# A decoder layer on one core: value and turning steps of the first attention reordered, first weight remainders on GpSimd, and routing logits by token rows

## The chip, the cores and the metric

One core of a Trainium2 chip runs the whole kernel. The metric is the device time in microseconds of one execution; the kernel before took 1061.29, 1063.31 and 1063.31 us in three runs, a median of 1063.31 us.

## The reference

The input is 16 sequences of 128 tokens with 256 features. One layer is computed, in float32:

```python
x = layernorm(x + attention(x))                    # 16 heads of 16, softmax over 128 keys, projection wo
x = layernorm(x + recurrence(k=x, v=ctx, w, u))    # out_t = A + exp(u + k_t) * (v_t * B + max(t - 1, 0))
                                                   # A = exp(-w)*A + exp(k_t)*v_t ; B = exp(w)*B + exp(-k_t), from t = 1 on
x = layernorm(x + experts(x))                      # 8 experts, each with all 128 tokens of a sequence:
# logits = x @ Wg.T (8 columns); gate = softmax(logits); sum_e gate[e] * (gelu(x @ W1[e] + b1[e]) @ W2[e] + b2[e])
```

Top-k takes 128 of 128 tokens, so each expert works on every token, weighted by its gate.

## The kernel before, in words

The sequences are worked on in eight pairs. A pair goes through attention, recurrence and routing (the numbered steps 1 to 62 of the `attend` and `route` functions), and then through eight visits, one for each expert. A visit streams the expert's two weight matrices in and runs units: `up` (TensorE, L578) makes hidden values, `hidden` (ScalarE, L728) applies gelu, `hidden_hi` and `hidden_lo` split the result in two parts, and `down` (L601) multiplies by the second matrix. Every engine has its own program with the same loops, and works strictly in the order in which its program is written; engines meet at semaphores.

Float32 products are made of three matmuls of a high and a low part (`product`, L405 to L409). So everything that TensorE reads is split: ScalarE copies the high part, and an engine subtracts it from the source for the low part. For weights these are `split_hi` (ScalarE, L739) and `split_lo` (VectorE, by the helper `low` at L790).

The first pair has nothing to run beside it. Its steps stand in the list FIRST_ORDER. The attention goes in four quarters (u = 0 to 3), each with two groups of four heads: scores (L407 to L409), the maximum and its subtraction (VectorE L856, L863), the exponential (ScalarE L674), turning the probabilities with eight transposes (TensorE L458), their high part (ScalarE L681) and low part (VectorE L870), the product with the values (TensorE L478, L479), and their sum, reciprocal and scaling (VectorE L876, L878, L880). There is one buffer of turned probabilities, and they are turned into PSUM banks 2 and 3. So the turning of a quarter stands behind the value product of the quarter before it in TensorE's program.

After attention come the projection, the first norm (L889, L808), the turning of y1, the exponentials (ScalarE L692 to L696), the two scans (VectorE L828), the mixture (L909, L911, L915, L919, with one addition on GpSimd at L1098), the turning back (TensorE L534), the second norm, and routing: part 0 turns x2 and splits it, part 1 makes the logits, part 2 turns them and subtracts the maximum, part 3 is the softmax, parts 4 and 5 turn the gates and add the gated b2 (L957). Routing of the first pair up to part 3 stands ahead of visit 0; parts 4 and 5 stand in the items of visit 0, beside the first steps of pair 1.

A visit with one active pair has 4 units and 8 items (three `up`, then `down` and `up` by turns); visit 0 is such a one, and the first 40 items carry the attention, recurrence and routing of pair 1, the next 48 those of pair 2. In each item an engine does the unit's part, then its steps of the next pair, then its splits of the coming weights. Seven of the eight weight pieces of visit 0 (all four of w1, three of w2) are split ahead of visit 0: ScalarE after steps Y1 and REC, VectorE at the same places.

SyncE issues all loads in one queue: 12 pieces at the start, then x and context of pair 1, then each further piece when the low part of the piece in its buffer is made.

The functions that the change touches:

## Time and profile before

| | us |
|---|---|
| runs | 1061.29, 1063.31, 1063.31 (median 1063.31) |
| profiled execution | 1064.93 |
| its span in the trace | 1063.2 |
| TensorE matmul busy | 946.8 |
| VectorE busy | 757.0 |
| ScalarE busy | 696.2 |
| GpSimd busy | 99.1 |

The profiled execution is 1.6 us above the median. Busy times are totals over stages with different limits: at the start, one engine after another works on the first pair; in the middle, TensorE is hardly ever idle.

### The profile page before, as it was taken

The numbers are of one execution on the slowest core, as the hardware profiler recorded it, in microseconds if no ns is written. First come the engines' busy times: TensorE is split into PE (matmuls) and PEld (weight loads), VectorE is DVE, ScalarE is ACT, GpSimd is POOL, SyncE is SP. The second block draws the span as 40 slices with busy tenths as digits, with TensorE's granted clock in tenths as the row PEclk, the third lists the DMA queues.
The fourth block names the chain that finished last, engine by engine and source line by source line (L and its number), as shares of the span: only waits on it lengthen the run. The fifth ranks groups of instructions, "written<-read, shape, count | busy, mean of one in ns | idle before, by whom it ended". The sixth has DMA issues, their size and how long they took to land.

```text
span 1063.2 us, 17552 instructions
## 1 busy us (share of the span) xinstructions
PE 946.8 (89%) x6480; PEld 850.4 (80%) x6480; DVE 757.0 (71%) x1526; ACT 696.2 (65%) x1231; POOL 99.1 (9%) x117
## 2 busy tenths in 40 slices
PE   6558687988799989999899989999899999999997
PEld 5447687878688878888798878988798888989997
DVE  6757768786688757787678758786678757655675
ACT  6347675665567766667677666677676665656775
POOL 2012001100120011100111001100011001000000
PEclk9669998999899999999999999999899999999999
DMA  6022233222122222222222222221222222232360
GB/s 200 11 70 89 90 109 100 80 60 70 51 80 71 79 70 80 67 83 80 70 90 70 71 90 63 69 88 61 79 80 80 61 69 80 87 112 90 103 186 11
DMA packets 89268, 86.40 MB, mean 81 GB/s; under 512 B 5960, under 2 KB 89184, under 8 KB 89184
## 3 DMA queue, kind: packets, MB, share of 16 engines
q1 hardware_dynamic: 89184, 85.29, 26.1%
q8 instruction: 52, 0.85, 0.3%
q14 instruction: 32, 0.26, 0.1%
HBM read 83.17 MB, written 2.10 MB: 80 GB/s over the span
## 4 chain that ended last, share of the span: by engine, by line
PE 65%; DVE 19%; ACT 11%; issue 4%; DMA 0%; POOL 0%; SPq 0%; ACTq 0%; POOLq 0%; DVEq 0%
PE up_ps L407 9%; PE up_ps L409 9%; PE up_ps L408 9%; PE down_ps L615 9%; PE down_ps L616 8%; PE down_ps L617 8%; DVE w_lo L790 4%; PE bank L407 3%; PE bank L408 3%; PE bank L409 3%; DVE h_lo L790 2%; ACT probs L674 2%; DVE pt_lo L870 2%; ACT L674 2%; DVE kd L820 1%
## 5 line engine op out<-in xcount | busy, mean ns | idle before, releaser
L728 ACT ACTIVATE h_all<-up_ps,b_all 128x512 f32<-128x512 f32 (+1 forms) x296 | 182.7, 632 | 292.6 <-PE up_ps L409 291.1
L615 PE MATMUL down_ps<-w_hi,h_hi 128*128 128x256 f32 x1024 | 299.9, 293 | 41.4 <-DVE h_lo L790 41.4
L790 DVE TENSOR_TENSOR w_lo<-w_raw,w_hi 128x512 fp32r<-128x512 f32 x296 | 206.1, 710 | 153.2 <-ACT w_hi L739 153.0
L616 PE MATMUL down_ps<-w_lo,h_hi 128*128 128x256 f32 x1024 | 293.7, 287 | 0.0
L617 PE MATMUL down_ps<-w_hi,h_lo 128*128 128x256 f32 x1024 | 293.6, 287 | 0.0
L615 PEld LDWEIGHTS down_ps<-w_hi,h_hi 128*128 128x128 f32 x1024 | 199.2, 194 | 54.1 <-DVE w_lo L790 39.7
L407 PE MATMUL up_ps<-x2t_hi,w_hi 128*128 128x512 f32 (+1 forms) x592 | 224.9, 380 | 0.0
L408 PE MATMUL up_ps<-x2t_lo,w_hi 128*128 128x512 f32 (+1 forms) x592 | 219.5, 371 | 0.0
L409 PE MATMUL up_ps<-x2t_hi,w_lo 128*128 128x512 f32 (+1 forms) x592 | 219.2, 370 | 0.0
L616 PEld LDWEIGHTS down_ps<-w_lo,h_hi 128*128 128x128 f32 x1024 | 200.0, 195 | 5.2
L790 DVE TENSOR_TENSOR h_lo<-h_all,h_hi 128x512 fp32r<-128x512 f32 x256 | 182.3, 712 | 27.6 <-ACT h_hi L719 27.6
L617 PEld LDWEIGHTS down_ps<-w_hi,h_lo 128*128 128x128 f32 x1024 | 199.9, 195 | 0.0
L739 ACT ACTIVATE w_hi<-w_raw 128x512 fp32r<-128x512 f32 x296 | 180.2, 628 | 0.7 <-PE down_ps L617 0.7
L719 ACT ACTIVATE h_hi<-h_all 128x512 fp32r<-128x512 f32 x256 | 160.8, 628 | 2.3
L409 PEld LDWEIGHTS up_ps<-x2t_hi,w_lo 128*128 128x128 f32 x592 | 114.6, 194 | 19.3
L407 PEld LDWEIGHTS up_ps<-x2t_hi,w_hi 128*128 128x128 f32 x592 | 116.2, 196 | 11.9
L408 PEld LDWEIGHTS up_ps<-x2t_lo,w_hi 128*128 128x128 f32 x592 | 116.2, 196 | 11.0
L1070 POOL TENSOR_TENSOR var_eps<-moments,eps_row 128x2 f32<-128x2 f32 x24 | 11.2, 466 | 667.3 <-DVE moments L801 667.3
L870 DVE TENSOR_TENSOR pt_lo<-bank,pt_hi 128x512 f16<-128x512 f32 x64 | 41.3, 684 | 30.0 <-ACT pt_hi L681 30.0
L972 DVE SCALAR_TENSOR_TENSOR acc<-down_ps,gate,acc 128x256 f32<-128x256 f32 x112 | 47.0, 475 | 13.1 <-PE down_ps L617 13.1
L820 DVE TENSOR_SCALAR kd<-k_both,head_mask 128x512 fp32r<-128x512 f32 x120 | 50.4, 478 | 0.0
L856 DVE TENSOR_REDUCE neg_max<-bank 128x4 f32<-128x512 f32 x58 | 38.1, 682 | 5.2 <-PE bank L409 5.2
(171 smaller groups left out, 1118.2 us busy)
## 6 DMA issues: line engine op xcount, KB each, us to landing
w_raw<-in_w_dram SPq DMA_DIRECT2D x296, 256.0 KB, 2.7
x_in<-in_x_dram SPq DMA_DIRECT2D x8, 256.0 KB, 3.0
ctx_sb<-in_ctx_dram SPq DMA_DIRECT2D x8, 256.0 KB, 3.1
out_dram<-acc SPq DMA_DIRECT2D x8, 256.0 KB, 3.2
w_raw<-in_wq_dram SPq DMA_DIRECT2D x1, 256.0 KB, 3.0
w_raw<-in_wk_dram SPq DMA_DIRECT2D x1, 256.0 KB, 4.2
w_raw<-in_wv_dram SPq DMA_DIRECT2D x1, 256.0 KB, 4.3
w_raw<-in_wo_dram SPq DMA_DIRECT2D x1, 256.0 KB, 4.6
```

The costliest lines, as they stand in the source:

```text
L407: nc.tensor.matmul(ps, hi, rhs_hi, start=first, stop=False)
L408: nc.tensor.matmul(ps, hi, rhs_lo, start=False, stop=False)
L409: return nc.tensor.matmul(ps, lo, rhs_hi, start=False, stop=last)
L615: nc.tensor.matmul(ps, hi, w2h[:, c, :], start=c == 0 and j == 0, stop=False, skip_group_check=True)
L616: nc.tensor.matmul(ps, hi, w2l[:, c, :], start=False, stop=False, skip_group_check=True)
L617: mm = nc.tensor.matmul(ps, lo, w2h[:, c, :], start=False, stop=c == FC - 1 and j == PAIR - 1, skip_group_check=True)
L719: nc.scalar.activation(h_hi[:, unit % HALF, :], h_all[:, unit % HALL, :], ACT.Copy).then_inc(h_hi_ready, 1)
L728: a = nc.scalar.activation(h_all[:, unit % HALL, k * wide:(k + 1) * wide], up_ps[unit % 2][:, k * wide:(k + 1) * wide], ACT.Gelu_apprx_tan ...
L739: nc.scalar.activation(piece((w1_hi, w2_hi)[i], i, q), raw(m, i), ACT.Copy)\
L790: return nc.vector.tensor_tensor(dst, src, hi.bitcast(F32), ALU.subtract)
L820: i = nc.vector.tensor_scalar(kd[:, :, :, h, :], k_both[:, :, c, :].rearrange("p a (j t) -> p a j t", j=PAIR), head_mask[:, h:h + 1], None ...
L870: nc.vector.tensor_tensor(pt_lo[:, i], by_head(bank[2 + i]), pt_hi[:, i], ALU.subtract)\
```

## The change

- Two buffers of turned probabilities (`pt_hi`, `pt_lo`). In the first attention odd quarters are turned into the PSUM banks `down_ps`, and the turning of each quarter stands ahead of the value product of the quarter before it. ScalarE's wait for the value product reaches back two quarters instead of one.
- The seven first weight splits: ScalarE's copies stand inside the first attention, and GpSimd does the subtractions.
- The addition of the recurrence that GpSimd made (L1098) is made by VectorE, for all pairs.
- Routing logits: the turned tokens become the stationary operand. For each of two sequences and two halves of the features there is one matmul with 16 moving columns (high and low part of Wg side by side) and one with 8 columns. The copy of the logits on ScalarE and their two transposes go; VectorE adds the two halves with one more reduction. This holds for all pairs.
- Parts 1 to 5 of the first pair's routing stand in items 1, 2, 3, 5 and 6 of visit 0, in the bank `down_ps[1]`. TensorE's wait for the b2 addition ahead of pair 1's values goes.
- Two memsets of padded Wg tiles go.

```diff
-        pt_hi = sb("pt_hi", [P, 2, HQ, S], F16)
-        pt_lo = sb("pt_lo", [P, 2, HQ, S], F16)
+        pt_hi = sb("pt_hi", [P, 2, 2, HQ, S], F16)
+        pt_lo = sb("pt_lo", [P, 2, 2, HQ, S], F16)
...
+        def route_bank(b, i):
+            return down_ps[1] if first(b) else bank[2 + i]
+        def turned(p, u):
+            return down_ps if first(p) and u % 2 else bank[2:4]
...
             def turn_probs(p, u):
+                if u == 1 and first(p):
+                    pe.wait_ge(shifted, 6)
...
-                    for kc in range(C):
-                        mm = product(bank[2][:, 0:TOK], wg_hi[:, kc, :], wg_lo[:, kc, :],
-                                     x2t_hi[:, kc, b % 3, :], x2t_lo[:, kc, b % 3, :], kc == 0, kc == C - 1)
-                    mm.then_inc(logits_t_ps, 1)
-                if part == 2:
-                    pe.wait_ge(logits_t_ready, b + 1)
                     for t in range(PAIR):
-                        mm = nc.tensor.transpose(bank[3][:, t * P:(t + 1) * P], logits_t[:, t * S:(t + 1) * S], ident[:])
+                        rows = slice(t * S, (t + 1) * S)
+                        ps = route_bank(b, 0)[:, t * 2 * E:(t + 1) * 2 * E]
+                        for kc in range(C):
+                            nc.tensor.matmul(ps, x2t_hi[:, kc, b % 3, rows], wg_both[:, kc].rearrange("p k e -> p (k e)"),
+                                             start=kc == 0, stop=False, skip_group_check=True)
+                            mm = nc.tensor.matmul(ps[:, 0:E], x2t_lo[:, kc, b % 3, rows], wg_both[:, kc, 0, :],
+                                                  start=False, stop=kc == C - 1, skip_group_check=True)
                     mm.then_inc(logits_ps, 1)
...
+                    if n == 0:
+                        for part in FIRST_ROUTE.get(k, []):
+                            route(0, part)
                     for p, s in steps(FIRST_ITEM[n] + k):
-                        if s in GATE_STEP:
+                        if s in GATE_STEP and p > 1:
                             route(p - 1, 4 + GATE_STEP.index(s))
...
-                            if u > 0:
-                                act.wait_ge(pv_ps, QUADS * p + (g - 1))
-                            nc.scalar.activation(pt_hi[:, i], by_head(bank[2 + i]), ACT.Copy).then_inc(pt_hi_ready, 1)
+                            if u > 1:
+                                act.wait_ge(pv_ps, QUADS * p + (g - 3))
+                            nc.scalar.activation(pt_hi[:, u % 2, i], by_head(turned(p, u)[i]), ACT.Copy).then_inc(pt_hi_ready, 1)
...
-                if part == 1:
-                    act.wait_ge(logits_t_ps, b + 1)
-                    nc.scalar.activation(logits_t, bank[2][:, 0:TOK], ACT.Copy).then_inc(logits_t_ready, 1)
...
                 if s == REC_STEP[3]:
+                    nc.vector.tensor_tensor(y1t[:], y1t[:], scan_a[:], ALU.add).then_inc(mix_a_ready, 1)
...
-                    lg = bank[3][:, 0:PAIR * P].rearrange("p (t e) -> p t e", t=PAIR)[:, :, 0:E]
-                    nc.vector.tensor_reduce(route_max[:], lg, AX_X, ALU.max, negate=True).then_inc(route_step, 1)
+                    halves = route_bank(b, 0)[:, 0:PAIR * 2 * E].rearrange("p (t k e) -> p t e k", t=PAIR, k=2)
+                    nc.vector.tensor_reduce(logits[:], halves, AX_X, ALU.add).then_inc(route_step, 1)
+                    dve.wait_ge(route_step, 5 * b + 1)
+                    nc.vector.tensor_reduce(route_max[:], logits[:], AX_X, ALU.max, negate=True).then_inc(route_step, 1)
...
-                if s == Y1_STEP:
-                    for q in range(G):
-                        split_lo(0, 0, q)
-                if s == REC_STEP[-1]:
-                    for q in range(G - 1):
-                        split_lo(0, 1, q)
...
-                if s == MIX_A_STEP:
-                    pool.wait_ge(xa_step, 6 * p + 3)
-                    pool.wait_ge(exps_ready, p + 1)
-                    nc.gpsimd.tensor_tensor(y1t[:], y1t[:], scan_a[:], ALU.add).then_inc(mix_a_ready, 1)
...
+            def split_lo(n, i, q):
+                m = sequence(n, i, q)
+                pool.wait_ge((w1_hi_ready, w2_hi_ready)[i], G * n + q + 1)
+                nc.gpsimd.tensor_tensor(piece((w1_lo, w2_lo)[i], i, q), raw(m, i), piece((w1_hi, w2_hi)[i], i, q).bitcast(F32),
+                                        ALU.subtract).then_inc((w1_ready, w2_ready)[i], 1)
...
-                EXP_STEP[0], EXP_STEP[1], TURN_STEP[0], EXP_STEP[2], SCORE_STEP[3], VALUE_STEP[0],
-                TURN_STEP[1], VALUE_STEP[1], EXP_STEP[3], TURN_STEP[2], VALUE_STEP[2], TURN_STEP[3], VALUE_STEP[3]]
-               + list(range(ATT_STEP, ROUTE_STEP[-1] + 1)))
+                EXP_STEP[0], EXP_STEP[1], TURN_STEP[0], EXP_STEP[2], SCORE_STEP[3], TURN_STEP[1],
+                VALUE_STEP[0], EXP_STEP[3], TURN_STEP[2], VALUE_STEP[1], TURN_STEP[3], VALUE_STEP[2], VALUE_STEP[3]]
+               + list(range(ATT_STEP, ROUTE_STEP[0] + 1)))
+FIRST_ROUTE = {1: [1], 2: [2], 3: [3], 5: [4], 6: [5]}
+FIRST_SPLIT = {EXP_STEP[1]: [(0, 0), (0, 1)], TURN_STEP[1]: [(0, 2), (0, 3)], EXP_STEP[3]: [(1, 0), (1, 1), (1, 2)]}
```

## Rows read from the trace of the kernel before

**Rows 1.** Busy time by engine (page, share of the span, instructions).

```profile
PE 946.8 (89%) x6480; PEld 850.4 (80%) x6480; DVE 757.0 (71%) x1526; ACT 696.2 (65%) x1231; POOL 99.1 (9%) x117
```

**Rows 2.** Busy time in a stretch: PE, PEld, DVE, ACT, POOL, granted clock, DMA share, GB/s.

```profile
30.00:42.00 12.00, 6.34 (x64) 5.13 (x64) 8.91 (x19) 4.08 (x8) 0.00 (x0) 0.55 0.01 3
```

**Rows 3.** Chain of waits, a turning in the first attention (start, length, what).

```profile
37.47 1.80 PE bank L458 x8
```

**Rows 4.** Timeline of VectorE in the first attention (start, length, what, idle before).

```profile
30.93 0.57 DVE L876 TENSOR_REDUCE pv_sum<-bank 128x136 f32<-128x408 f32 x1
...
31.99 1.28 DVE L870 TENSOR_TENSOR pt_lo<-bank,pt_hi 128x512 f16<-128x512 f32 x2
...
42.03 0.29 DVE L880 TENSOR_TENSOR att<-pv_sum,inv_sum 128x128 f32<-128x128 f32 x1
```

**Rows 5.** Timeline of ScalarE: turned probabilities, weight copies.

```profile
25.61 1.07 ACT L681 ACTIVATE pt_hi<-bank 128x512 f16<-128x512 f32 x2
...
44.88 2.18 ACT L739 ACTIVATE w_hi<-w_raw 128x512 fp32r<-128x512 f32 x4
```

**Rows 6.** Timeline of VectorE from the first norm to the second.

```profile
55.18 0.66 DVE L901 TENSOR_TENSOR inc_a<-exp_k,ctx_t 128x504 f32<-128x504 f32 x1
...
58.00 1.63 DVE L911 TENSOR_TENSOR exp_k<-exp_k,ramp 128x512 f32<-128x512 f32 x1
...
61.01 1.89 DVE L790 TENSOR_TENSOR w_lo<-w_raw,w_hi 128x512 fp32r<-128x512 f32 x3
```

**Rows 7.** Timeline of ScalarE, last of the exponentials' copies.

```profile
54.46 0.62 ACT L696 ACTIVATE y1t<-bank 128x512 f32<-128x512 f32 x1
```

**Rows 8.** GpSimd's subtraction of values, and its addition for pair 0.

```profile
20.47 1.16 POOL L1090 TENSOR_TENSOR v_all<-v_all,v_cat 128x512 f32<-128x512 f32 x1
...
57.32 1.77 POOL L1098 TENSOR_TENSOR y1t<-y1t,inc_a 128x512 f32<-128x512 f32 x1 [6.52 <-DVE inc_a L828]
```

**Rows 9.** VectorE beside GpSimd's addition of pair 2, and line 911's durations (min/median/max).

```profile
276.69 1.76 DVE L909 TENSOR_TENSOR exp_k<-ctx_t,inc_b 128x512 f32<-128x512 f32 x1
...
L911 DVE TENSOR_TENSOR exp_k<-exp_k,ramp x8: 691/693/1633, 58.0 to 889.4; 128x512 f32<-128x512 f32 x8
```

**Rows 10.** Timeline of TensorE from the first turning back to pair 1's first projection.

```profile
61.14 1.12 PE L534 MATMUL bank<-ident,exp_k 128*128 128x128 f32 x4 [8.39 <-DVE exp_k L919]
...
68.19 0.55 PE L407 MATMUL bank<-x2t_hi,wg_hi 128*128 128x256 f32 x1 [1.02 <-DVE x2t_lo L790]
...
75.43 0.36 PE L407 MATMUL bank<-xt_hi,proj_hi 128*128 128x256 f32 x1
```

**Rows 11.** Timeline of VectorE: the last small instruction of routing's part 3.

```profile
72.57 0.17 DVE L790 TENSOR_TENSOR gate_all<-gate,gate_all 128x16 fp32r<-128x16 f32 x1
```

**Rows 12.** VectorE in visit 0: the idle times at both ends of a full stretch.

```profile
80.69 0.69 DVE L790 TENSOR_TENSOR w_lo<-w_raw,w_hi 128x512 fp32r<-128x512 f32 x1 [4.21 <-ACT w_hi L739]
...
94.24 0.69 DVE L856 TENSOR_REDUCE neg_max<-bank 128x4 f32<-128x512 f32 x1 [0.59 <-PE bank L409]
```

**Rows 13.** ScalarE: a table load in visit 0 and its idle time ahead of pair 1's exponential.

```profile
87.62 1.28 ACT L674 ACT_TABLE_LOAD   x1
91.86 1.23 ACT L674 ACTIVATE probs<-probs 128x512 f32<-128x512 f32 x2 [2.95 <-DVE probs L863]
```

**Rows 14.** TensorE: transposes, and the value products with 51 and 34 columns.

```profile
23.49 1.04 PE L458 MATMUL bank<-ident,probs 128*128 128x128 f32 x8
...
28.22 0.18 PE L478 MATMUL bank<-v_cat,pt_hi 128*128 128x51 bf16 x1
28.25 0.18 PE L479 MATMUL bank<-v_cat,pt_lo 128*128 128x34 bf16 x1
```

**Rows 15.** Weight loads of pair 2's logits matmuls.

```profile
292.10 0.19 PEld L407 LDWEIGHTS bank<-x2t_hi,wg_hi 128*128 128x128 f32 x1
292.22 0.19 PEld L408 LDWEIGHTS bank<-x2t_lo,wg_hi 128*128 128x128 f32 x1
```

**Rows 16.** TensorE ahead of pair 2's turning back.

```profile
281.77 1.12 PE L534 MATMUL bank<-ident,exp_k 128*128 128x128 f32 x4 [4.46 <-DVE exp_k L919]
```

More of the change, by code:

```diff
@@ L457, in turn_probs @@
                     for h in range(HQ):
-                        mm = nc.tensor.transpose(by_head(bank[2 + i])[:, h, :], probs[:, u % 2, i, h, :], ident[:])
+                        mm = nc.tensor.transpose(by_head(turned(p, u)[i])[:, h, :], probs[:, u % 2, i, h, :], ident[:])
                     mm.then_inc(pt_ps, 1)
@@ L567, in route @@
                     for t in range(PAIR):
-                        mm = nc.tensor.matmul(by_tile(bank[3])[:, t, :], gate_t[:, t * S:(t + 1) * S], b2_all[:], start=True, stop=True)
+                        mm = nc.tensor.matmul(by_tile(route_bank(b, 1))[:, t, :], gate_t[:, t * S:(t + 1) * S], b2_all[:], start=True, stop=True)
                     mm.then_inc(b2_ps, 1)
@@ L774, in _ @@
                         hidden(n, u)
+                    if n == 0:
+                        for part in FIRST_ROUTE.get(k, []):
+                            route(0, part)
                     for p, s in steps(FIRST_ITEM[n] + k):
-                        if s in GATE_STEP:
+                        if s in GATE_STEP and p > 1:
                             route(p - 1, 4 + GATE_STEP.index(s))
@@ L956, in route @@
                     dve.wait_ge(b2_ps, b + 1)
-                    nc.vector.tensor_tensor(x2_all[:, b % 2], by_tile(bank[3]), x2_all[:, b % 2], ALU.add).then_inc(x2_biased, 1)
+                    nc.vector.tensor_tensor(x2_all[:, b % 2], by_tile(route_bank(b, 1)), x2_all[:, b % 2], ALU.add).then_inc(x2_biased, 1)
             def hidden_lo(n, u):
@@ L1003, in _ @@
             nc.vector.memset(ones[:], 1.0).then_inc(dve_setup, 1)
+            dve.wait_ge(dve_setup, 1)
+            nc.vector.tensor_tensor_scan(ramp[:], ones[:], ones[:], 0.0, ALU.mult, ALU.add).then_inc(dve_setup, 1)
             dve.wait_ge(dve_setup, 2)
-            nc.vector.tensor_tensor_scan(ramp[:], ones[:], ones[:], 0.0, ALU.mult, ALU.add).then_inc(dve_setup, 1)
-            dve.wait_ge(dve_setup, 3)
             nc.vector.tensor_scalar(ramp[:], ramp[:], -2.0, 0.0, ALU.add, ALU.max)
@@ L1013, in _ @@
                 attend(0, s)
-                if s == Y1_STEP:
-                    for q in range(G):
-                        split_lo(0, 0, q)
-                if s == REC_STEP[-1]:
-                    for q in range(G - 1):
-                        split_lo(0, 1, q)
                 if s == ATT_STEP:
@@ L1022, in _ @@
                     dve.wait_ge(masks_made, MASKS + 2)
-                    low(wg_lo[:, :, 0:E], wg_raw[:], wg_hi[:, :, 0:E])
-                    nc.vector.tensor_scalar(b2_rest[:], b2_raw[:], third[:, 0:1], None, ALU.mult)
+                    low(wg_both[:, :, 1, :], wg_raw[:], wg_both[:, :, 0, :])
+                    nc.vector.tensor_scalar(b2_raw[:], b2_raw[:], third[:, 0:1], None, ALU.mult)
                     nc.vector.tensor_scalar(third[:, 1:2], third[:, 0:1], -2.0, 1.0, ALU.mult, ALU.add).then_inc(dve_setup, 1)
                     dve.wait_ge(dve_setup, DVE_SETUP - 2)
-                    nc.vector.scalar_tensor_tensor(out=b2_all[:], in0=b2_hi[:].bitcast(F32), scalar=third[:, 1:2], in1=b2_rest[:],
+                    nc.vector.scalar_tensor_tensor(out=b2_all[:], in0=b2_hi[:].bitcast(F32), scalar=third[:, 1:2], in1=b2_raw[:],
                                                    op0=ALU.mult, op1=ALU.add).then_inc(dve_setup, 1)
@@ L1047, in _ @@
                         hidden_lo(n, order[k - 1][1])
+                    if n == 0:
+                        for part in FIRST_ROUTE.get(k, []):
+                            route(0, part)
                     for p, s in steps(FIRST_ITEM[n] + k):
-                        if s in GATE_STEP:
+                        if s in GATE_STEP and p > 1:
                             route(p - 1, 4 + GATE_STEP.index(s))
@@ L1125, in _ @@
                 attend(0, s)
+                for i, q in FIRST_SPLIT.get(s, []):
+                    split_lo(0, i, q)
             for n in range(VISITS):
```

40 lines of the change are left out of this document (16 added, 24 removed).

## The prediction

> **What bounds the kernel now.** I read the page's busy times first: TensorE is busy for 89% of the span, VectorE for 71%, ScalarE for 65% [rows 1]. That is an average. The table of stretches shows the other case: from 30 to 42 us TensorE works 6.3 of 12 us at a granted clock of 0.55, hence mostly at 1.2 GHz, and VectorE 8.9 [rows 2]. There one pair goes through its attention alone, and each engine waits for the next. The chain of waits shows eight transposes that take 1.80 us at this clock [rows 3]; they stand behind a value product, which stands behind VectorE's low part, so turning, copying and subtracting follow each other. All that follows is coupled by the written order of the items, and no engine waits for a weight load after the first 10 us. So what the first pair loses or gains, I take to move the end by as much.
>
> **First attention.** VectorE has no idle time to speak of up to 30.93, where the last subtraction of maxima ends, and its part ends with the scaling at 42.03+0.29 = 42.3 [rows 4]. In between it does four groups of sum, reciprocal and scaling, each 1.06 (30.93 to 31.99), and six low parts, 0.6 each: 4.2+3.6 = 7.8 us of work in 11.4 us. The reordered list takes the waits out, so VectorE could be done at 38.8. But ScalarE now does seven weight copies there, 0.54 each [rows 5]. I laid its program out by its own durations: copies from 25.6, the first turned copy at 26.7 (its reader VectorE comes at 27.35, no loss), then exponentials, two copies, exponentials, three copies, and so the third quarter's turned copy at 33.7, its first half ready at 34.3. VectorE is there at 33.2 and waits 1.1. End at 39.9. I add 0.1 for blocking by GpSimd (below): **gain 2.3**. Bounds: 3.5 (ScalarE hides it all) and 0.5 (VectorE is blocked too).
>
> **Weight remainders.** The four subtractions that VectorE did ahead of the scans bring nothing: the multiplication at 55.18 waits for ScalarE's last copy, which ends at 54.46+0.62 = 55.08 [rows 6, 7]. The three at 61.01, 0.6 each, keep the norm's statistics until 62.81 [rows 6]; the transposes that these need end at 61.14+1.12 = 62.26 [rows 10]. **Gain 0.5.** On GpSimd each costs 1.16 to 1.77 [rows 8]; seven fit between 26 and 37 us and nobody reads them before visit 0, 65 us at the earliest: zero on the path. Their buffers are free sooner, so SyncE's reloads, which waited for them in its one queue until 52, go from the context load (about 42) on; nothing waits for a load, so zero either way.
>
> **The recurrence's addition.** Line 911 takes 0.69 in the median but 1.63 in the first pair, while GpSimd's addition runs from 57.32 to 59.09; for pair 2 it is line 909, of the same form, that takes 1.76 [rows 8, 9]. One VectorE instruction is thus stretched by 0.94 to 1.08 in each pass. VectorE's own addition costs 0.60, the distance of such instructions. For the first pair that is a **gain of 0.34**. By this sum the logits' inputs are ready 2.3+0.5+0.34 = 3.1 us sooner. The Trainium skill (SBUF — State Buffer, Who interferes with whom) says the same in general: a VectorE instruction with two SBUF inputs and a GpSimd one lock each other out for a whole instruction. The rows agree, and the rule speaks against the seven subtractions beside the attention. What it would hit: VectorE's inputs there lie mostly in PSUM; only the scalings have two in SBUF. Two of four meet a subtraction, up to 1.16 each [rows 8]; the first of them falls mostly into the 1.1 us wait.
>
> **Start of visit 0.** Before, 7.24 us pass from the logits' matmul at 68.19 to pair 1's first projection at 75.43 [rows 10]. Now TensorE has: `up` 0, 12 matmuls at 1.2 GHz, 256/1.2 = 213 ns each, 2.56; four transposes at 0.225, 0.9 [rows 3]; `up` 1, a quarter at the low and the rest at the high level, 1.7; the new logits, 0.9. Sum 6.1, a **gain of 1.1** (0 if the clock stays low through `up` 1).
>
> **Routing inside visit 0.** In VectorE's program from 80.69 on the first idle time is at 94.24, 0.59 us [rows 12]. The small routing instructions, the last of which ran at 72.57 while it was idle otherwise [rows 11], now stand in that full stretch: 0.17 and some 0.03 of start each, the softmax part's six (one pair closer) 1.07, the maximum part with one more reduction 0.6. **Loss 1.67.** The b2 addition (0.6) falls into the idle 0.59, since TensorE waits there for the shifted scores: zero, or 0.6 without that cover. ScalarE must load its table for the exponential and again for gelu, 2x1.28+0.2 = 2.8 us; it has 2.95 us idle ahead of pair 1's exponential, where it waits for VectorE [rows 13], and it runs some 3 us ahead of VectorE at that item: zero, at most 2.8. TensorE's new wait for the gates (item 5) has pair 1's scores behind it, and these wait for VectorE's masked keys, made later still: zero.
>
> **Other pairs.** Each loses the 1.08 block and gets 0.60. For pairs 1 and 2 VectorE sets the pace (TensorE waits 4.46 us for it ahead of the turning back [rows 16]): 2x0.48, **gain 1.0**. For the last five TensorE is full, and I count 0.1 each, **gain 0.5** (0 to 2.4). The logits: out go six matmuls of 256 columns at 0.12 and two transposes at 0.11 (eight in 1.04, less the tail) [rows 14], 0.94; in come eight narrow ones. Their price isn't in the trace. From below: matmuls of 51 and 34 columns with 16-bit weights start 0.03 apart (28.22, 28.25); from above, the load of 0.19 and a matmul of 0.18 one after the other, 0.37 [rows 14, 15]. I take 0.11, the transposes' distance, as they too load 128 columns of float32 each time. 8x0.11 = 0.88, **gain 0.06 a pair, 0.4 in seven**. The copy that goes from ScalarE (0.39) and VectorE's extra reduction (0.2) lie beside full TensorE: zero.
>
> **Sum.** -2.3-0.5-0.34-1.1+1.67-1.0-0.5-0.4 = -4.4 us. The profiled execution had 1064.93 (span 1063.2), so 1060.5 against that; the median of the runs is 1.6 lower, 1063.31, and against it I forecast **1058.9**.
>
> **Rivals.**
>
> A. The narrow matmuls are cheap. For it: the 0.03 distance [rows 14]. Against: those weights have 16 bits, these 32. At 0.04 to 0.06, 64 of them bring 3.2 to 4.5 more: about 1055.
>
> B. VectorE is blocked by GpSimd in the first attention at two or more scalings [rows 8], behind ScalarE's late copies; 1.1 to 2.2 more on the path: 1060 to 1061.
>
> C. Visit 0 takes back more: the table loads aren't covered, or TensorE, waiting longer for keys, falls to 1.2 GHz and runs a `down` at 2.56 instead of 1.4. For it: this stage already shows waits on all engines. 2.2 more: 1061.1.
>
> D, slower. Each narrow matmul waits for its own load: 0.37 instead of 0.11. It decides in TensorE's full stages, in routing part 1. 64x0.26 = 17 us, so 1063.3-4.4+16.6 = 1075.5; it outweighs the rest from 0.11+4.4/64 = 0.18 a matmul on. Against it: the loads of the old logits start 0.12 apart beside running matmuls on the same rows of the array [rows 15], each 0.19 long, so they are hidden, and behind transposes of 128 columns they still are. The Trainium skill (TensorE: Matmul & The Clock Gate, The mechanism) has the rule behind this rival: a weight load overlaps running matmuls only when the row group differs. The rows here contradict it.
>
> E. No effect: the head's gain is real but is lost again in a later wait. Against: nothing later is tied to a fixed time.
>
> **How the numbers follow.** Forecast 0.48, A 0.15, B 0.14, C 0.14, D 0.05, E 0.04. About 0.2% (2.1 us) is what a measurement can tell from no change. Forecast, A, B and half of C are faster, 0.83 (I count a little off for what I missed: 0.82); the other half of C and E the same, 0.12; D and unnamed mishaps slower, 0.06. The range takes in A's middle and C: 1055.0 to 1062.0; left out are D, E and the ends.
>
> **What would show it.** The last scaling of the first attention ends near 40 us; VectorE waits about 1 us for the third quarter's turned copy; line 911 takes 0.69 in all eight passes, and no VectorE instruction 1.7 beside them; `up` 0 starts near 65, pair 1's projection near 71; VectorE's full stretch in visit 0 ends near 95 instead of 98; narrow matmuls start 0.11 apart. I am wrong if TensorE's busy time grows by over 5 us, if VectorE's scalings in the attention take 1 us and more, or if the start of visit 1 lies where it was.

## The result and the profile after

The changed kernel took 1054.41 us (median of four runs, 1053.62 to 1056.16), the kernel before in the same comparison 1062.8 us: a ratio of 0.9926, interval 0.9908 to 0.9943, which is 7.9 us less of 1063.3. Two later comparisons gave 0.9931 and 0.9926. I had forecast 4.4 us less. The direction was right, the size was not, and the time lies below my range (1055.0 to 1062.0). In the two later comparisons the medians of the changed kernel were 1056.57 and 1055.48 us, just inside the range, but the distance to the kernel before was the same 7.3 to 7.9 us. The profiled execution had 1053.62 us, span 1051.9. It is the lowest of its four runs, and that of before lies 1.6 above the median, so the two traces differ by 11.3 us where the medians differ by 8.4.

The page's busy times after, beside [rows 1]:

```profile
span 1051.9 us, 17529 instructions
PE 935.5 (89%) x6480; PEld 842.3 (80%) x6480; DVE 751.3 (71%) x1533; ACT 694.9 (66%) x1225; POOL 94.6 (9%) x116
```

TensorE's 946.8 us went down by 11.3, but such a total also counts how long the clock stayed low. So I go by places. The timeline of VectorE after, at the end of the first attention (start, duration, operation; in brackets the idle time before it and what ended it), answers to [rows 4]:

```profile
32.07 0.57 DVE L878 TENSOR_REDUCE pv_sum<-bank 128x136 f32<-128x408 f32 x1
32.92 1.24 DVE L882 TENSOR_TENSOR att<-pv_sum,inv_sum 128x128 f32<-128x128 f32 x1
34.08 1.27 DVE L872 TENSOR_TENSOR pt_lo<-bank,pt_hi 128x512 f16<-128x512 f32 x2
36.12 0.54 DVE L882 TENSOR_TENSOR att<-pv_sum,inv_sum 128x128 f32<-128x128 f32 x1
38.61 0.29 DVE L882 TENSOR_TENSOR att<-pv_sum,inv_sum 128x128 f32<-128x128 f32 x1
39.67 0.29 DVE L882 TENSOR_TENSOR att<-pv_sum,inv_sum 128x128 f32<-128x128 f32 x1
...
55.61 0.69 DVE L913 TENSOR_TENSOR exp_k<-exp_k,ramp 128x512 f32<-128x512 f32 x1
...
59.63 0.76 DVE L798 BATCH_NORM_STATS2 stats<-bank 128x6 f32<-128x256 f32 x2 [1.21 <-PE bank L538]
```

The last scaling ends at 39.96, where I had 39.9, but on another way. (In the two further traces of the changed kernel it ends at 38.79 and 39.03, since the attention starts 1.1 and 0.7 us sooner there; its length is the better measure, see run e5.) VectorE doesn't wait for the third quarter's copy at all: the low parts at 34.08 have no idle time before them. Instead the first scaling takes 1.24 instead of 0.29 and the second 0.54, and GpSimd's row says why:

```profile
26.24 2.52 POOL L1101 TENSOR_TENSOR w_lo<-w_raw,w_hi 128x512 fp32r<-128x512 f32 x2 [2.39 <-ACT w_hi L743]
30.27 6.24 POOL L1101 TENSOR_TENSOR w_lo<-w_raw,w_hi 128x512 fp32r<-128x512 f32 x5 [1.51 <-ACT w_hi L743]
```

Its five subtractions run back to back from 30.27 to 36.51, and both stretched scalings lie in there; those at 38.61 and 39.67 don't. One of my signs for being wrong has thus come: a scaling in the attention that takes 1 us and more. The second norm's statistics wait for TensorE's transposes now and no longer stand behind three subtractions: the step of 0.5 I had counted.

The start of visit 0 on TensorE, which answers to [rows 10]:

```profile
64.92 0.58 PE L410 MATMUL up_ps<-x2t_hi,w_hi 128*128 128x256 f32 x1 [0.93 <-DVE x2t_lo L792]
...
69.58 0.17 PE L556 MATMUL down_ps<-wg_both,x2t_hi 128*128 128x16 f32 x1
69.60 0.25 PE L558 MATMUL down_ps<-wg_both,x2t_lo 128*128 128x8 f32 x1
69.71 0.26 PE L556 MATMUL down_ps<-wg_both,x2t_hi 128*128 128x16 f32 x1
69.82 0.25 PE L558 MATMUL down_ps<-wg_both,x2t_lo 128*128 128x8 f32 x1
...
70.38 0.36 PE L410 MATMUL bank<-xt_hi,proj_hi 128*128 128x256 f32 x1
```

`Up` 0 starts at 64.92 (forecast near 65), the projection at 70.38 (near 71), and the narrow matmuls stand 0.11 apart. From `up` 0 to the projection it is 5.46 us, in two further traces of the changed kernel 6.57 and 6.80, where I had worked out 6.1. Then VectorE's full stretch, beside [rows 12]:

```profile
75.66 0.69 DVE L792 TENSOR_TENSOR w_lo<-w_raw,w_hi 128x512 fp32r<-128x512 f32 x1 [5.12 <-ACT w_hi L743]
...
92.40 1.89 DVE L792 TENSOR_TENSOR w_lo<-w_raw,w_hi 128x512 fp32r<-128x512 f32 x3
94.20 0.88 DVE L977 SCALAR_TENSOR_TENSOR acc<-down_ps,gate,x 128x256 f32<-128x256 f32 x2
...
101.59 0.58 DVE L878 TENSOR_REDUCE pv_sum<-bank 128x136 f32<-128x408 f32 x1
```

In the trace before, these four stand at 80.69, 96.05, 97.85 and 106.64. The lead is 5.03 us at the first and 3.65 at the accumulation: the routing in the stretch costs 1.38 there, near my 1.67. But at the sum of pair 1's values the lead is 5.05 again. Either the loss was given back, or the trace before lost as much in the same place; run e4 decides it.

### The profile page after: what moved, and what is told of

It reads as the page before. It is cut to its first block, busy times and chain, and to the rows that moved or that the text cites. A ratio compares the mean times of both kernels' runs of the same rounds, so it can differ in the third digit from the quotient of the medians.

```text
span 1051.9 us, 17529 instructions
## 1 busy us (share of the span) xinstructions
PE 935.5 (89%) x6480; PEld 842.3 (80%) x6480; DVE 751.3 (71%) x1533; ACT 694.9 (66%) x1225; POOL 94.6 (9%) x116
## 4 chain that ended last, share of the span: by engine, by line
PE 67%; DVE 17%; ACT 11%; issue 3%; DMA 0%; POOL 0%; SPq 0%; ACTq 0%; POOLq 0%; DVEq 0%
PE up_ps L410 10%; PE up_ps L412 10%; PE up_ps L411 10%; PE down_ps L619 9%; PE down_ps L621 9%; PE down_ps L620 9%; PE bank L410 3%; PE bank L411 2%; DVE w_lo L792 2%; PE bank L412 2%; DVE pt_lo L872 2%; ACT probs L681 2%; DVE h_lo L792 2%; ACT L681 2%; DVE kd L822 2%
## 5 line engine op out<-in xcount | busy, mean ns | idle before, releaser
L792 DVE TENSOR_TENSOR w_lo<-w_raw,w_hi 128x512 fp32r<-128x512 f32 x289 | 195.3, 688 | 151.4 <-ACT w_hi L743 151.1
L411 PE MATMUL up_ps<-x2t_lo,w_hi 128*128 128x512 f32 (+1 forms) x592 | 218.4, 369 | 0.0
L872 DVE TENSOR_TENSOR pt_lo<-bank,pt_hi 128x512 f16<-128x512 f32 x60 | 38.5, 684 | 26.0 <-ACT pt_hi L688 26.0
```

Source lines behind the costliest of these rows:

```text
L411: nc.tensor.matmul(ps, hi, rhs_lo, start=False, stop=False)
L792: return nc.vector.tensor_tensor(dst, src, hi.bitcast(F32), ALU.subtract)
L872: nc.vector.tensor_tensor(pt_lo[:, u % 2, i], by_head(turned(p, u)[i]), pt_hi[:, u % 2, i], ALU.subtract)\
```

## The experiments

Each was timed in five rounds. The ratios are against the kernel before, on the same chip; times in us are ratios times 1063.5. The interval of one ratio is about 1.4 us to either side, so two kernels that differ by less than 1.5 to 2 us are not told apart. The changed kernel was run again in the first and the third group, as a0 and a1. A diff shows what an experiment changes in the changed kernel, for b1 and b2 in the kernel before; those of e2, e5, b1, h1 and g1 are shortened, partly to words.

**First group: the changed kernel again, the addition back on GpSimd, the old logits, and routing ahead of visit 0.**

> The changed kernel once more, beside the others on one chip, for its level and for how far its trace repeats itself. Theory 1 (the surplus over my 4.4 us is real and lies in terms that I sized too small): 7.5 to 9 us below the kernel before, and the lead over the kernel before grows at the same places in a second trace: 3.3 us when the first pair's logits inputs are ready, 5 at the end of visit 0, and by some 0.3 to 0.6 in each later pair. Theory 2 (half of the surplus is a clock that fell in other places by chance): 5 to 7 us below, and the later steps of 0.6 us and more come at other places than in the first trace.

Run a0: 0.9931 (0.9917 to 0.9946), 7.3 us less than before. The size stands.

```diff
-                    nc.vector.tensor_tensor(y1t[:], y1t[:], scan_a[:], ALU.add).then_inc(mix_a_ready, 1)
+                if s == MIX_A_STEP:    # GpSimd's program
+                    pool.wait_ge(xa_step, 6 * p + 3)
+                    pool.wait_ge(exps_ready, p + 1)
+                    nc.gpsimd.tensor_tensor(y1t[:], y1t[:], scan_a[:], ALU.add).then_inc(mix_a_ready, 1)
```

> The changed kernel with the recurrence's addition back on GpSimd, for all pairs. By my sum this term was 0.34 + 1.0 + 0.5 = 1.8 us, so 1.8 us slower than the changed kernel. If the surplus lies here (the block of one VectorE instruction by GpSimd costs its full 1.1 us less 0.6 in every pair, and more where it makes TensorE fall to 1.2 GHz), 3 to 5 us slower. If the later pairs do not care, 0.3 us. VectorE should again show one instruction of 1.6 to 1.8 us in each pass.

Run e1: 0.9964 (0.9951 to 0.9977): 3.5 us slower than the changed kernel, where my sum had 1.8 for the addition. The block is back in every pass:

```profile
513.57 1.65 POOL L1097 TENSOR_TENSOR y1t<-y1t,inc_a 128x512 f32<-128x512 f32 x1 [18.94 <-DVE inc_a L830]
```

```profile
513.99 1.78 DVE L792 TENSOR_TENSOR w_lo<-w_raw,w_hi 128x512 fp32r<-128x512 f32 x1
```

```diff
# in words
-    per sequence and half: matmul with 16 columns (wg_both), matmul with 8 columns
+    per half: product(wg_hi, wg_lo, x2t_hi, x2t_lo), three matmuls of 256 columns
+    ScalarE: activation(logits_t, ..., ACT.Copy); TensorE, part 2: two transposes of logits_t
-    VectorE: tensor_reduce(logits, halves, add)
```

> The changed kernel with the old logits (six matmuls of 256 columns, a copy on ScalarE, two transposes), the first pair's still inside visit 0. By my sum 0.4 us slower in seven pairs and about 0.2 us in visit 0: 0.6 us. If the surplus lies here, because the old form also holds TensorE's program at a wait for ScalarE in each pair: 2.5 to 4 us slower, and TensorE's distance around the transposes is over 0.3 us.

Run e2: 0.9953 (0.9937 to 0.9969): 2.3 us slower than the changed kernel, where I had 0.4 to 0.6. A good part of it lies in one place. TensorE in this kernel at pair 2's logits:

```profile
287.15 0.28 PE L419 MATMUL bank<-x2t_hi,wg_lo 128*128 128x256 f32 x1
287.91 0.44 PE L566 MATMUL bank<-ident,exp_uk 128*128 128x128 f32 x2 [0.47 <-DVE h_lo L803]
```

and in the changed one:

```profile
284.69 0.17 PE L556 MATMUL bank<-wg_both,x2t_hi 128*128 128x16 f32 x1
...
285.39 0.25 PE L558 MATMUL bank<-wg_both,x2t_lo 128*128 128x8 f32 x1
285.50 0.36 PE L619 MATMUL down_ps<-w_hi,h_hi 128*128 128x256 f32 x1
```

The two transposes need ScalarE's copy of the logits. Mostly a `down` stands between the product and the transposes and hides it. In this pair's item the transposes come right behind the product, and TensorE stands for 0.76 us from one start to the next instead of 0.12 (the trace names VectorE's h_lo as releaser, yet h_lo is not what a transpose of logits reads). The changed logits have no transposes and so no stop. Before, the same stop is there from 292.81 to 293.56.

```diff
-               + list(range(ATT_STEP, ROUTE_STEP[0] + 1)))
-FIRST_ROUTE = {1: [1], 2: [2], 3: [3], 5: [4], 6: [5]}
+               + list(range(ATT_STEP, ROUTE_STEP[-1] + 1)))
+FIRST_ROUTE = {0: [4], 1: [5]}
```

> The changed kernel with parts 1 to 3 of the first pair's routing again ahead of visit 0, parts 4 and 5 in its first two items. By my sum this move gained 1.1 us at the start and lost 1.67 us in VectorE's full stretch, so without it the kernel is 0.3 to 0.6 us FASTER or the same. Theory 3 (VectorE's full stretch in visit 0 does not set the end; what it loses there is given back at the next stage, where TensorE runs at the high clock): 1 to 2 us SLOWER than the changed kernel, as the gain at the start stands alone.

Run e4: 0.9931 (0.9916 to 0.9947), the changed kernel's own ratio. I had expected the same or 0.3 to 0.6 us faster. The trace shows both halves of the trade: the projection starts later, at 72.83, and the full stretch is shorter. Here VectorE's stretch starts 2.46 us later than after and the accumulation only 0.42 later:

```profile
78.12 0.69 DVE L792 TENSOR_TENSOR w_lo<-w_raw,w_hi 128x512 fp32r<-128x512 f32 x1 [4.49 <-ACT w_hi L743]
...
94.62 0.87 DVE L977 SCALAR_TENSOR_TENSOR acc<-down_ps,gate,x 128x256 f32<-128x256 f32 x2
97.67 0.69 DVE L872 TENSOR_TENSOR pt_lo<-bank,pt_hi 128x512 f16<-128x512 f32 x1 [2.18 <-ACT pt_hi L688]
...
102.55 0.58 DVE L878 TENSOR_REDUCE pv_sum<-bank 128x136 f32<-128x408 f32 x1
```

From the first of these lines to the sum of pair 1's values it is 24.43 us, in the changed kernel 25.93 (75.66 to 101.59). So the loss by the routing is not given back: 1.49 us of it are still there at that sum. What balances it is the gain at the start. From the first matmul on x2 to the first of these lines e4 takes 13.17 us, the three traces of the changed kernel 10.73, 11.84 and 12.07. The two cancel to within 1 us, and so that part of the change is worth nothing by itself, within 2 us.

**Second group: the old order of values and turning, the splits on VectorE, and two parts of the change put alone into the kernel before.**

```diff
-                EXP_STEP[0], EXP_STEP[1], TURN_STEP[0], EXP_STEP[2], SCORE_STEP[3], TURN_STEP[1],
-                VALUE_STEP[0], EXP_STEP[3], TURN_STEP[2], VALUE_STEP[1], TURN_STEP[3], VALUE_STEP[2], VALUE_STEP[3]]
+                EXP_STEP[0], EXP_STEP[1], TURN_STEP[0], EXP_STEP[2], SCORE_STEP[3], VALUE_STEP[0],
+                TURN_STEP[1], VALUE_STEP[1], EXP_STEP[3], TURN_STEP[2], VALUE_STEP[2], TURN_STEP[3], VALUE_STEP[3]]
```

> The changed kernel with the first attention's turnings and value products in the old order; the two buffers, the copies inside the attention and GpSimd's subtractions stay. My sum (the waits go, less ScalarE's late copies) makes the order worth 2.3 us, so 2.3 us slower than the changed kernel or a little more, since ScalarE's copies then delay the old order too; TensorE again shows transposes behind each value product and the last scaling ends near 42 to 43 us. If most of the head's gain came from the moved subtractions, under 1 us slower.

Run e3: 0.9969 (0.9959 to 0.9979): 4.0 us slower than the changed kernel by a0's ratio, 4.6 by the two others, where I had 2.3 or a little more. The last scaling ends at 42.36+0.29 = 42.65, and the waits are back:

```profile
31.44 0.89 DVE L882 TENSOR_TENSOR att<-pv_sum,inv_sum 128x128 f32<-128x128 f32 x1
34.10 0.58 DVE L878 TENSOR_REDUCE pv_sum<-bank 128x136 f32<-128x408 f32 x1 [0.57 <-PE bank L484]
34.95 1.12 DVE L882 TENSOR_TENSOR att<-pv_sum,inv_sum 128x128 f32<-128x128 f32 x1
37.84 0.58 DVE L878 TENSOR_REDUCE pv_sum<-bank 128x136 f32<-128x408 f32 x1 [0.57 <-PE bank L484]
```

I measure the attention from VectorE's first subtraction of maxima to the end of the last scaling (the wait for TensorE's scores ahead of that subtraction differs by up to 0.48 us from trace to trace of one kernel). It takes 21.61 us here, against 18.63 to 18.82 in three traces of the changed kernel and 20.95 in the kernel before. So the order alone is worth 2.8 to 3.0 us there. With the old order back but the moved splits left, this kernel's attention is 0.7 longer than the old one: the moved splits cost about that much in the old order. The rest of the 4 us isn't in the attention; 1.5 us of it, in this one trace, are a fall of TensorE's clock in visit 0 (the table in the next section).

```diff
-                for i, q in FIRST_SPLIT.get(s, []): split_hi / split_lo   # ScalarE in the attention, GpSimd
+                if s == Y1_STEP:        # ScalarE and VectorE, as before
+                    for q in range(G): split(0, 0, q)
+                if s == REC_STEP[-1]:
+                    for q in range(G - 1): split(0, 1, q)
```

> The changed kernel with the seven first weight splits at their old places, copies on ScalarE after steps Y1 and REC and subtractions on VectorE. By my sum it loses 0.5 us at the second norm's statistics and wins back what ScalarE's copies and GpSimd's block cost in the attention (1.1 us wait and 0.1): 0.7 us FASTER than the changed kernel. In the changed kernel's trace the first scaling took 1.24 instead of 0.29 us and the second 0.54, so the rival that GpSimd blocks VectorE gives the same sign: 1.2 less 0.5. If neither is right and the moved subtractions bring what they are meant to, 0.5 to 1 us slower.

Run e5: 0.992 (0.9908 to 0.9933), 8.5 us less than before and the lowest ratio of all. No scaling is stretched, nothing waits, and the attention takes 17.45 us, 1.2 to 1.4 less than in the changed kernel:

```profile
34.17 0.29 DVE L886 TENSOR_TENSOR att<-pv_sum,inv_sum 128x128 f32<-128x128 f32 x1
34.38 1.28 DVE L876 TENSOR_TENSOR pt_lo<-down_ps,pt_hi 128x512 f16<-128x512 f32 x2
36.42 0.29 DVE L886 TENSOR_TENSOR att<-pv_sum,inv_sum 128x128 f32<-128x128 f32 x1
37.47 0.29 DVE L886 TENSOR_TENSOR att<-pv_sum,inv_sum 128x128 f32<-128x128 f32 x1
...
56.17 1.89 DVE L796 TENSOR_TENSOR w_lo<-w_raw,w_hi 128x512 fp32r<-128x512 f32 x3
57.98 0.75 DVE L802 BATCH_NORM_STATS2 stats<-bank 128x6 f32<-128x256 f32 x2
```

The price stands there as well: the three subtractions delay the statistics by some 0.5 us. Moving the splits into the attention thus gains 0.5 and costs about 1.3, near the 1.2 that I had. By the ratios e5 is 0.6 to 1.2 us faster than the changed kernel, which the intervals don't separate.

```diff
+                    nc.vector.tensor_tensor(y1t[:], y1t[:], scan_a[:], ALU.add).then_inc(mix_a_ready, 1)
-                if s == MIX_A_STEP:   # GpSimd's three waits-and-add lines go; kernel before, nothing else
```

> The kernel before with this one edit: the recurrence's addition on VectorE. My sum: 1.8 us below the kernel before. From putting it back into the changed kernel (3.5 us slower): 2.7 to 3.5 us below, of which 0.34 in the first pair, 0.5 each in pairs 1 and 2 and 0.27 each in the last five, where the distances around the four turning-back transposes shrink from 0.86 to 0.60 us, would make 2.7.

Run b1: 0.9977 (0.9968 to 0.9985), 2.4 us less than before. With 0.9 us to either side this fits both my sum of 1.8 and the 2.7 that I had read from the trace.

> The kernel before with this one edit: logits by token rows in all pairs, routing of the first pair still ahead of visit 0. My sum: 0.4 us in seven pairs; in the first pair, which has nothing beside it, the copy and the transposes go too (2.09 us from the first logits matmul to the transposes becomes 0.9 to 1.7, and 0.34 for the transposes), so 1 to 1.5 us: together 1.5 to 2 us below the kernel before. If TensorE's stop at the transposes in pair 2 (0.75 us ahead of them) also goes, 2.5 us.

Run b2, the kernel before with the new logits alone (the edit is the logits' part of the change): 0.9987 (0.9978 to 0.9997), 1.4 us less, where I had 1.5 to 2.5. The first pair brings nothing in its trace: from the first logits matmul to pair 1's projection it takes 7.52 us, before 7.24.

**Third group: the changed kernel again, the head alone, and two other places for the splits.**

> The changed kernel a third time, as the measure for the three others of this call. 6.5 to 8 us below the kernel before. Its trace tells how far the leads over the kernel before in the middle of the run repeat: if a step of 0.5 to 1 us is the clock's, it comes at another pair than in the two traces at hand; the 0.27 at each of the last five turning-backs must repeat.

Run a1: 0.9926 (0.9913 to 0.9939), 7.9 us less.

> The changed kernel with both edits that reach all pairs undone (addition on GpSimd, old logits): what is left is the new order of the first attention, the moved splits and the routing inside visit 0. If the effects add, it lies 7.3 - 2.4 - 1.4 = 3.5 us below the kernel before by the single edits to the kernel before, and 7.3 - 3.5 - 2.3 = 1.5 us below by the single undoings in the changed one. By my sum without these terms: 2.3 + 0.5 + 1.1 - 1.67 + 0.2 = 2.2 to 2.4 us. 3.5 would put half of the surplus in the head, 1.5 would put it all in the other pairs. The head's own trace, with 5 us at the end of visit 0, speaks for 3.5 and more.

Run e6, both edits of all pairs undone (the diffs of e1 and e2 together): 0.9964 (0.995 to 0.9977), 3.8 us less than before. What the first pair and visit 0 bring is thus 3.8, by my terms (2.3+0.5+1.1-1.67) 2.2; the two edits together are worth 4.0 (0.9964 against 0.9926), by my terms 2.2.

```diff
-                for i, q in FIRST_SPLIT.get(s, []): split_lo(0, i, q)   # GpSimd
+                if s == Y1_STEP: ...        # VectorE's split_lo, as before; ScalarE's copies stay in the attention
```

> The changed kernel with only GpSimd's seven subtractions back on VectorE at the old places, ScalarE's copies stay inside the first attention. It separates the two costs of the moved splits. If GpSimd's block is the cost (first scaling 1.23 and second 0.54 instead of 0.29 us), both scalings take 0.29, VectorE waits some 0.6 us for the third quarter's turned copy, the last scaling ends 0.6 us sooner, and the second norm's statistics start 0.5 us later: the same time as the changed kernel. If ScalarE's copies are the cost (1.1 us wait, as I had it), the last scaling ends where it was and the kernel is 0.5 us slower.

Run h1: 0.9941 (0.9928 to 0.9955), 6.3 us less, 1.6 slower than the changed kernel, which the intervals don't quite separate. The trace shows the wait that I had forecast, freed of the block that hid it:

```profile
33.01 0.29 DVE L882 TENSOR_TENSOR att<-pv_sum,inv_sum 128x128 f32<-128x128 f32 x1
33.91 1.29 DVE L872 TENSOR_TENSOR pt_lo<-bank,pt_hi 128x512 f16<-128x512 f32 x2 [0.61 <-ACT pt_hi L688]
35.96 0.29 DVE L882 TENSOR_TENSOR att<-pv_sum,inv_sum 128x128 f32<-128x128 f32 x1
```

At this place ScalarE's copies make VectorE 0.61 late and GpSimd's block 0.95, and the two overlap. The whole attention, from the first subtraction of maxima on, takes:

| kernel | copies | subtractions | attention, us |
|---|---|---|---|
| e5 | outside | outside | 17.45 |
| h1 | inside | outside | 18.14 |
| changed (three traces) | inside | inside, GpSimd | 18.63, 18.77, 18.82 |

ScalarE's copies cost 0.7, and GpSimd's subtractions 0.5 to 0.7 on top. Down to the second norm's split there is little left between h1 and the changed kernel (48.94 and 48.70 us from the split of q on), so most of the 1.6 in their times is not explained by the attention. In these two traces it lies in visit 0, where h1's shows the low clock from 89 to 92 us and takes 1.55 us longer (next section); whether the other executions of h1 do the same isn't known.

```diff
-                for i, q in FIRST_SPLIT.get(s, []): ...
+                if s == CTX_STEP: ...   # ScalarE: all seven copies; GpSimd: the three of w2
+                if s == Y1_STEP: ...    # VectorE: the four of w1
```

> A version meant to beat both: the seven copies on ScalarE after the context's copy (it is idle there for 7 us), the four w1 subtractions on VectorE at the old place (where they are hidden under ScalarE's exponentials), the three w2 subtractions on GpSimd beside the projection, where VectorE waits. No block and no wait in the attention, no 0.5 us at the second norm: 1.2 + 0.5 = 1.7 us below the changed kernel, 0.5 below the one with all splits on VectorE. If GpSimd's subtractions are still running when its square root for the first norm is due, that norm starts up to 1 us later and the version only equals it.

Run g1: 0.9934 (0.992 to 0.9947), 7.0 us less, no better than the changed kernel. Its attention takes 17.45 us like e5's, as meant. What it gained there it lost here:

```profile
41.83 3.96 DVE L1036 TENSOR_SCALAR decay_row<-ones,decay 128x128 f32<-128x128 f32 x4
45.82 0.69 DVE L894 TENSOR_TENSOR y<-bank,x_bo 128x512 f32<-128x512 f32 x1
```

```profile
41.72 3.79 POOL L1107 TENSOR_TENSOR w_lo<-w_raw,w_hi 128x512 fp32r<-128x512 f32 x3 [18.49 <-ACT w_hi L743]
```

Four small operations with one tensor input, 0.86 us together after, take 3.96 beside GpSimd's three subtractions, and the residual sum behind them comes 5.52 us after the start of the split of the context instead of 3.77 us. The Trainium skill (SBUF — State Buffer, Who interferes with whom) counts such a `tensor_scalar` among the operations that can take the shared port pair; this trace agrees, with 3.1 us for four. I had looked at operations with two inputs alone.

**Where the all-pair edits pay.** In each trace I read the starts of the transposes that turn the mixture back, once for each of pairs 0 to 7, and took the distances (us):

| kernel | addition | logits | 0 to 1 | 1 to 2 | 2 to 3 | 3 to 7 (four) | 7 to the end |
|---|---|---|---|---|---|---|---|
| before | GpSimd | old | 109.7 | 110.9 | 122.4 | 488.4 | 170.6 |
| e6 | GpSimd | old | 108.9 | 109.8 | 122.3 | 487.3 | 170.7 |
| b1 | VectorE | old | 110.1 | 110.5 | 122.0 | 486.4 | 170.6 |
| e2 | VectorE | old | 108.5 | 109.9 | 122.0 | 485.9 | 170.6 |
| b2 | GpSimd | new | 109.2 | 109.8 | 121.2 | 488.4 | 170.8 |
| e1 | GpSimd | new | 109.2 | 109.7 | 121.2 | 488.8 | 170.8 |
| after | VectorE | new | 107.1 | 108.8 | 121.0 | 485.8 | 170.7 |
| changed, second | VectorE | new | 109.0 | 109.9 | 120.9 | 487.0 | 170.7 |
| changed, third | VectorE | new | 108.7 | 108.8 | 121.0 | 487.0 | 170.8 |

Two columns are clear. From pair 2 to 3 every kernel with the old logits has 122.0 to 122.4 and every one with the new 120.9 to 121.2: the logits bring 1.1 us in this one stage, where the stop was, and nothing that shows in the four full stages after. There it is the addition: 487.3 to 488.8 with it on GpSimd (mean 488.2), 485.8 to 487.0 on VectorE (mean 486.4), hence 0.45 a pair. The first two columns don't show the 1.0 us that I had counted for pairs 1 and 2: from pair 0 to pair 2 it is 220.6 in before and in b1, 218.6 and 218.4 in e6 and e2, while the changed kernel itself scatters from 215.9 to 218.9. Part of the 0.45 can be pointed at. TensorE before, at pair 3's turning back:

```profile
403.72 0.40 PE L409 MATMUL up_ps<-x2t_hi,w_lo 128*128 128x512 f32 x1
404.17 0.66 PE L534 MATMUL bank<-ident,exp_k 128*128 128x128 f32 x4
404.58 0.36 PE L615 MATMUL down_ps<-w_hi,h_hi 128*128 128x256 f32 x1
```

and after:

```profile
395.17 0.40 PE L412 MATMUL up_ps<-x2t_hi,w_lo 128*128 128x512 f32 x1
395.41 0.60 PE L538 MATMUL bank<-ident,exp_k 128*128 128x128 f32 x4
395.77 0.36 PE L619 MATMUL down_ps<-w_hi,h_hi 128*128 128x256 f32 x1
```

0.45+0.41 = 0.86 us from the matmul before the transposes to the one behind them, then 0.24+0.36 = 0.60. All five full passes show it, with 0.86 to 0.88 before and in e1, and 0.59 to 0.60 after. The waits of 0.2 us carry no name in the trace, since they are short, but they go with the addition and with nothing else.

## Why the prediction was right or wrong

The forecast was too small, 4.4 us for 7.3 to 7.9. (Its terms add up to 4.47, and the chances that I summed to 0.83 make 0.84; neither matters.)

**The other pairs: the step that failed.** I gave the addition 0.1 in each of the last five pairs because TensorE is full there. It was 0.27 at the turning back itself and 0.45 by the stages' distances, so about 2.1 instead of 0.5: 0.3 from pair 2 to 3 and 1.8 in the four behind. A full TensorE hides what VectorE does only if VectorE is ahead at that item; at the turning back it is not, by 0.2 us. I gave the logits 0.06 a pair, 0.4 in all; it was right for the full stages, and it missed the stop of 0.75 us in pair 2 that was in the trace before, right behind the rows of the loads that I had read. There the transposes' removal brings 1.1. Together 2.3 us of the missing 2.9 to 3.5. The runs of single edits agree in direction: 2.4 and 3.5 for the addition (my sum 1.8), 1.4 and 2.3 for the logits (0.4). Only 0.27 of the 0.45 is located; where the rest arises isn't shown.

**Routing inside visit 0: the loss came and stayed, and the trace before hid it.** Forecast 1.67; against the trace before 1.38 at the accumulation and nothing at the sum of pair 1's values. But that trace is a poor measure at this place. After a stretch with 1.12 of 3 us busy, TensorE ran at half its clock there, 1.2 GHz:

```profile
90.00:93.00 3.00, 1.12 (x4) 0.96 (x5) 3.00 (x7) 1.15 (x3) 2.77 (x4) 0.93 0.50 172
93.00:96.00 3.00, 3.00 (x13) 2.72 (x13) 2.41 (x5) 1.89 (x3) 1.04 (x1) 0.50 0.37 91
```

(from, to, length, busy times of PE, PEld, DVE, ACT and POOL, granted clock, DMA share, GB/s.) Pair 1's scores and the `down` behind them lay in it: that `down` takes 2.32 us (94.00 to 96.32), in e4 at the full clock 1.43. All traces, from VectorE's line at the start of the full stretch (80.69 before, 75.66 after) to the sum of pair 1's values, fall into groups:

| traces | pair 0's routing | low clock at those scores and `down` | us |
|---|---|---|---|
| b2, e4 | ahead | no | 24.42, 24.43 |
| before, b1 | ahead | yes | 25.95, 25.99 |
| changed (three), e1, g1 | inside | no | 25.91 to 25.93 |
| e2, e6 (old logits) | inside | no | 25.71, 25.72 |
| e3, e5, h1 | inside | yes | 27.46 to 27.49 |

The routing costs 1.5 and the fall of the clock costs 1.5, each with and without the other. At the accumulation the routing's loss is 2.04 against e4: 0.52 and 0.98 for the small instructions, and 0.60 for the b2 addition, which I had put at zero because of the idle 0.59 in [rows 12]. That idle time stood in the low clock of the trace before; neither e4 nor the changed kernel has it. Then 0.55 comes back, as VectorE waits less for ScalarE's turned copy (1.62 for 2.18 us), and 1.49 stays. So it was right to carry a loss on, at least to this sum. At the start the move gains 1.1 to 2.4 against e4, so that as a whole it is worth about zero; my net loss of 0.57 lies within that scatter. The table loads' price (rival C) didn't come: ScalarE makes both, at 77.94 and 79.98, 1.28 each, and still stands idle for 2.06 us ahead of pair 1's exponential at 88.33, waiting for VectorE. The clock's half of rival C shows in e3, e5 and h1, but just so in the trace before.

Against the two traces with the low clock the changed kernel thus gains what the clock took there. Whether before falls at this place in most of its executions is open, since it has one trace; b1, the nearest kernel, falls too, b2 doesn't. The changed kernel doesn't in three traces, though in its second and third the clock fell from 83 to 86 us, where nothing hung on it. The stretches are, after and then third:

```profile
83.00:86.00 3.00, 2.50 (x16) 1.93 (x15) 3.00 (x8) 2.98 (x6) 1.24 (x1) 1.00 0.00 1
```

```profile
83.00:86.00 3.00, 3.00 (x9) 2.01 (x9) 3.00 (x8) 2.98 (x6) 1.27 (x1) 0.50 0.02 5
```

One kernel, the same place, either level. So a single trace must not be read to 1 us.

**First attention: right in size, partly wrong in way.** The attention became 2.1 to 2.3 us shorter (20.95 before, 18.63 to 18.82 in the changed kernel) for my 2.3. The order's gain is a little less than I said (2.8 to 3.0 in e3 against 3.5), the deduction of 1.2 was right in sum (1.2 to 1.4 against e5), but in the trace it was the block of GpSimd (0.95 and 0.25) and not ScalarE's lateness that spent it. I had said that the first block falls into ScalarE's wait: it does, only it is the longer of the two (h1: 0.61). Rival B, a price of 1.1 or more at two scalings, thus happened, but in place of the wait and not behind it.

**The rest of the head.** From the first turning back to the first matmul on x2 it is 7.05 us before and 6.44 after, for my 0.5 at the second norm; TensorE's wait ahead of that turning back is 0.3 shorter (8.39 in [rows 10], 8.1 in the traces with the addition on VectorE), for my 0.34; the operation that was line 911 (now 913) takes 0.69 in all eight passes. The start of visit 0 brought 1.78, 0.67 and 0.44 in the three traces of the changed kernel (7.24 less 5.46, 6.57 and 6.80), 0.96 in the mean, for my 1.1: the clock rises at another moment each time, 2.8, 5.3 and 5.7 us behind the start of `up` 0 by the granted clock.

**Rival D** is refuted: behind the first two of each group of eight, all 48 narrow matmuls start 0.11 us after the one before, with loads of 0.19 each. The rule that I weighed (the Trainium skill, TensorE: Matmul & The Clock Gate, The mechanism), taken alone, is contradicted by the trace; the same section also names a background weight buffer into which a load may go ahead of running matmuls, and with that the trace is compatible. A wait for each load would have cost 17 us by my sum. **Rival A** is refuted by the same rows.

Summed again with measured terms: 4.5, plus 1.6 for the addition and 0.7 for the logits, makes 6.8. From the first matmul on x2 to the sum of pair 1's values, where I had a net loss of 0.57, the three traces of the changed kernel are 1.0 us shorter in the mean (36.66, 37.76 and 37.99 for 38.45). That is 1.5 more, the size of the clock's fall in the trace before: 8.3 with it, against 7.3 to 7.9 measured. Run e6, with 3.8 for my 2.2, fits the larger figure. **What stays open** is whether that 1.5 belongs to the medians or only to these traces. All these are terms from single traces, and by the mean granted clock (0.955 to 0.962) TensorE stood at its low level for some 80 to 95 us of each of these four, at places that differ from run to run of the same kernel; the trace called after has the least of it. The table's 3-to-7 column holds 485.8 and 487.0 for one kernel. The 1.0 for the addition in pairs 1 and 2 isn't shown either. The three versions of where the splits stand (changed, h1, g1) lie within 1.6 us and aren't ordered by these runs.

## What to carry to other kernels

When an engine moves work beside a critical stretch, ask for each of its instructions with whom it shares SBUF's ports: here seven subtractions were hidden but stretched two scalings by 1.2 us in all, and the version that keeps copies and subtractions out of the stretch is as fast or faster. In a stage where one engine is full, don't price an edit on another engine at nothing: look at each place where the full engine stands for 0.2 to 0.8 us, for it is those that recur in every pair. To price one edit inside a stage, compare traces that differ in that edit alone, and look at the granted clock of both: here a fall of the clock in the one trace hid a loss of 1.5 us in the other.

## What was not expected of the hardware

- Four `tensor_scalar` operations of 128x128 with one tensor input took 3.96 us instead of 0.86 beside GpSimd's subtractions of 1.2 to 1.3 us each, as strongly blocked as those with two inputs (0.29 to 1.24).
- A float32 matmul with 16 or 8 moving columns starts 0.11 us behind the one before it, like a transpose of 128 columns, and is recorded with 0.25; matmuls of 256 columns beside it start 0.12 apart. With a new load of 128 columns for each, narrower operands bring next to nothing here.
- TensorE's clock did not fall at fixed places of the program: behind a stretch (80 to 83 us) with 1.09 of 3 us busy in both, it was granted 1.00 in one trace of the changed kernel and 0.50 in another.
